# A seventh tap of the third channel block computed on ScalarE and GpSimd, one chunk late

## The reference

```
x = x + linear_attention(_gn(x))                 # layer 0
t = conv1x1(_gn(x), w_in)                        # layer 1, 384 channels
t = irfft2(rfft2(8x8 patches of t) * fft_filter)
t = depthwise_conv3x3(t, w_dw)                   # nine taps a channel
x = x + conv1x1(gelu(t[:192]) * t[192:], w_out)  # layer 1, end
```

## Time and profile before

| | |
|---|---|
| median of 3 runs | 3679.16 us (3678.93 to 3683.74) |
| the profiled execution | 3683.6 us, span 3681.8 us |
| mean granted TensorE clock | 0.977 |
| PE busy | 3441.9 us, 93% |
| DVE busy | 3143.5 us, 85% |
| POOL busy | 2025.3 us, 55% |
| ACT busy | 1658.8 us, 45% |

### The profile page before, as it was taken

How to read it: one execution, slowest core, us unless ns; L and a number is a source line. 1 busy time by engine, 2 the same in 40 slices (tenths; PEclk the granted TensorE clock), 3 DMA queues, 4 the chain that set the end, 5 groups by cost and what they waited for, 6 DMA issues and landing times.

```text
span 3681.8 us, 50526 instructions
## 1 busy us (share of the span) xinstructions
PE 3441.9 (93%) x17974; PEld 2995.9 (81%) x17974; DVE 3143.5 (85%) x4800; ACT 1658.8 (45%) x2834; POOL 2025.3 (55%) x1295
## 2 busy tenths in 40 slices
PE   4999999999999999999999999999999999999998
PEld 4987779877898778977789777897779977799775
DVE  7987989879898798987989869898798987989878
ACT  1433744337443374424744246442564325643265
POOL 2554655546555465564655646556465564655554
PEclk9999999999999999999999999999999999999999
DMA  6205232143321433123321233312332133321422
GB/s 216 69 26 172 100 115 70 38 160 112 104 69 60 146 114 110 61 69 129 129 95 61 87 123 120 101 59 95 121 121 95 52 121 109 115 87 52 145 95 95
DMA packets 185483, 369.92 MB, mean 100 GB/s; under 512 B 7915, under 2 KB 8979, under 8 KB 184979
## 3 DMA queue, kind: packets, MB, share of 16 engines
q1 hardware_dynamic: 185234, 366.68, 29.2%
HBM read 265.99 MB, written 100.66 MB: 100 GB/s over the span
## 4 chain that ended last, share of the span: by engine, by line
PE 32%; DVE 14%; issue 4%; POOL 2%; ACT 2%; DMA 0%; DVEq 0%; ACTq 0%; POOLq 0%; SPq 0%
DVE bank L970 6%; PE bank L1104 6%; PE bank L1103 6%; PE bank L1108 6%; PE bank L1133 2%; PE bank L1288 2%; PE bank L1261 2%; PE bank L1254 2%; DVE nrm L871 1%; DVE qt_lo L891 1%; PE bank L1121 1%; DVE xr L901 1%; PE bank L1273 1%; PE bank L1080 1%; DVE xr L904 1%
## 5 line engine op out<-in xcount | busy, mean ns | idle before, releaser
L445 POOL TENSOR_TENSOR t<-t 128x768 f32<-128x768 f32 x256 | 536.6, 2096 | 512.8 <-DVE t L807 512.8
L1103 PE MATMUL bank<-w_hi,x_hi 128*128 128x384 f32 x2304 | 778.9, 338 | 4.0 <-ACT x_hi L553 4.0
L1104 PE MATMUL bank<-w_lo,x_hi 128*128 128x384 f32 x2304 | 779.7, 338 | 0.0
L438 POOL TENSOR_TENSOR x_lo<-xa,x_hi 128x512 fp32r<-128x512 f32 x360 | 492.1, 1383 | 519.8 <-ACT x_hi L553 519.8
L970 DVE SCALAR_TENSOR_TENSOR bank<-big,wdw,bank 128x512 f32<-128x512 f32 x1072 | 753.8, 745 | 23.8 <-PE bank L1288 20.9
L558 ACT ACTIVATE t<-t 128x768 f32<-128x768 f32 x256 | 217.1, 848 | 867.9 <-POOL t L445 867.9
L510 POOL TENSOR_TENSOR prod<-prod 128x512 f32<-128x512 f32 x320 | 410.9, 1284 | 320.9 <-ACT prod L650 302.2
L817 DVE SCALAR_TENSOR_TENSOR kt<-t 128x384 f32<-128x384 f32 x256 | 534.9, 2090 | 0.0
L1108 PE MATMUL bank<-w_hi,x_lo 128*128 128x384 f32 x2304 | 533.1, 339 | 0.5 <-POOL x_lo L438 0.5
L1103 PEld LDWEIGHTS bank<-w_hi,x_hi 128*128 128x128 f32 x2304 | 434.7, 189 | 6.7 <-ACT x_hi L553 4.4
L1104 PEld LDWEIGHTS bank<-w_lo,x_hi 128*128 128x128 f32 x2304 | 433.8, 188 | 0.3
(11 more groups left out here) (132 smaller groups left out, 6969.9 us busy)
## 6 DMA issues: line engine op xcount, KB each, us to landing
xr<-x SPq DMA_DIRECT2D x128, 768.0 KB, 4.6
xa<-x SPq DMA_DIRECT2D x64, 768.0 KB, 6.3
x_scratch<-xr SPq DMA_DIRECT2D x64, 768.0 KB, 3.5
xa<-x_scratch SPq DMA_DIRECT2D x64, 768.0 KB, 6.1
xr<-x_scratch SPq DMA_DIRECT2D x64, 768.0 KB, 4.8
out<-xr SPq DMA_DIRECT2D x64, 768.0 KB, 3.5
big<-x SPq DMA_DIRECT2D x8, 768.0 KB, 10.0
w_raw<-wqkv_t SPq DMA_DIRECT2D x1, 1728.0 KB, 7.0
```

Source lines behind the costliest of these rows:

```text
L438: nc.gpsimd.tensor_tensor(dst, src, hi, ALU.subtract).then_inc(s_lo, 1)
L445: nc.gpsimd.tensor_tensor(a, a, b[:, :, ::-1, :], ALU.add).then_inc(s_add, 1)
L1103: nc.tensor.matmul(dst, hi(k), whi(k), start=first and k == 0, stop=False)
L1104: nc.tensor.matmul(dst, hi(k), wlo(k), start=False, stop=False)
```

## The change

The third block gets a seventh tap (q = 6) from ACT and POOL, and DVE begins it at (7,2). Tap 6 reads the row below the chunk, so its product cannot be formed in the step of the other six; it is formed at the start of the next step, on ACT by `product(c - 2, 6)` and on POOL by `add_product(c - 2, 6)`, both ahead of that step's other work. `copy_t` of tile 0 goes ahead of the products 0 to 2, and product 0, which overwrites slot 0, waits for tap (7,2) in place of (6,2). DVE's late taps are reordered.

```diff
-POOL_TAPS = 6
+POOL_TAPS = 7
-LATE = [(6, 2), (6, 0), (7, 2), (7, 0), (8, 2), (8, 0), (6, 1), (7, 1), (8, 1)]
+LATE = [(6, 0), (7, 0), (7, 2), (8, 0), (8, 2), (6, 1), (7, 1), (8, 1)]
-LAST = [(6, 2), (6, 0), (7, 2), (7, 0), (8, 2), (8, 0), (6, 1), (7, 1), (8, 1)]
+LAST = LATE
...
+                    if c >= 2:
+                        add_product(c - 2, 6)
                     if within(edge, 0, NCH, -1):
-                        for q in range(1, POOL_TAPS - 1):
+                        for q in range(1, 5):
                             add_product(c - 1, q)
...
-                            act.wait_ge(s_dw, dw_count(i, c - 1, (6, 2)))
+                            act.wait_ge(s_dw, dw_count(i, c - 1, (7, 2)))
...
+                    if gated:
+                        if c < NCH + 1:
+                            act.wait_ge(s_img, (i * 8 + c - 1) * 4 + 6)
+                        product(c - 2, 6)
+                    if tile:
+                        copy_t(T, 0)
                     if conv:
                         for q in range(3):
                             product(c - 1, q, edge == 1)
-                    if tile:
-                        copy_t(T, 0)
...
-                        for m, early in enumerate((LAST[0:2], LAST[2:4], LAST[4:6])):
+                        for m, early in enumerate((LAST[0:2], LAST[2:4], LAST[4:5])):
...
                         dve.wait_ge(s_img, T + 2)
-                        tap(c - 2, 6, 2)
                         tap(c - 2, 6, 0)
-                        tap(c - 2, 7, 2)
+                        tap(c - 2, 7, 0)
                     if 3 <= c <= NCH:
                         add_out(3, 2)
                     if gated:
-                        tap(c - 2, 7, 0)
+                        tap(c - 2, 7, 2)
+                        tap(c - 2, 8, 0)
                         tap(c - 2, 8, 2)
-                        tap(c - 2, 8, 0)
                         tap(c - 2, 6, 1)
```

More of the change, by code:

```diff
@@ L526, in part_c @@
                     if within(edge, 0, NCH, -1):
-                        add_product(c - 1, POOL_TAPS - 1)
+                        add_product(c - 1, 5)
                     if within(edge, 0, NCH if i + 1 < images else NCH - 1):
@@ L1014, in part_c @@
                             rope((i + 1) * NT, 0, 0)
-                        for q, k in LAST[6:]:
+                        for q, k in LAST[5:]:
                             tap(c - 2, q, k, last)
```

## The result

The changed kernel took 3673.25 us in the median of 16 runs (3664.39 to 3677.66), the kernel before 3680.36 us in runs beside them. The ratio is 0.9978, with a 95% interval of 0.997 to 0.9986: 0.22% faster, where 0.47% was forecast (3662.0 us). The profiled execution took 3674.24 us with a span of 3672.3 us, 9.5 us less than the span of before.

The account below looks back on a forecast made before the run. DVE was taken to set nearly the whole step of part C, with PE as floor near 17.8 us. 8 x (3.3 - 1.0 - 0.15) = 17.2 us off the median 3679.2 gave 3662.0 us; range 3654 to 3680, the forecast's own 3655 to 3671.

Parts of the forecast that it names:

- The steady step: Part C's repeating step, 18.67 us: a gain of 0.66 in each of five steps, 3.3 us an image.
- The ties: Four near-equal arrivals in the steady step, at (7,2), `gelu`, `copy_t` 3 and the output blocks, each reckoned to a tenth.
- the further 0.08 that I took off: Steady step: gain lowered from 0.74 to 0.66 us because four ties can only cost.
- the loop over product 6, POOL and the output block: Steady step: product 6, its add, (7,2), six POOL instructions and the output block form a loop of about 17.9 us.
- The lower bound of the range: 3654 us: a step gain of 0.9 with 0.8 lost at c = 2, 30 us in all.
- the 0.15 of the image's end: End of each image: the 4 us wait goes without a gain because `g_lo` ends 1.2 later; counted as -0.15 us.
- the 0.31 for the form with `prod`: Steady step: DVE's tap reading `prod` no longer runs beside POOL's `low_part`, 0.97 - 0.66 = 0.31 us gained.
- The step c = 2, up to `gelu`: First chunk: product 6 and its add delay the `gelu` table load; loss 1.34 or 0.8 us, mean 1.0 an image.
- Nothing behind gives it back: Step c = 2: the 1.34 us by which the `gelu` table load moves later is not recovered afterwards.
- The ties did not slip: Rival, chance 0.20: steady-step hand-overs cost 0.35 more or (7,2) stays long; only 4.8 us gained, 3674 us.
- DVE did bound the step before: Denies a rival, chance 0.05: PE's floor is higher, gain under 0.25 a step, time 3679 us.
- POOL did not make the step longer: Denies a rival, chance 0.15: POOL's chain behind product 0 becomes the bound, step 19.0 us, 21 us slower, 3700 us.

Follow-up runs that it names:

- The reorder alone: Kernel before with only DVE's late taps reordered, (6,2) second and (7,2) behind `add_out(3, 2)`, all nine taps kept on DVE: 3676.28 us, ratio 0.9997.
- The delay in the kernel before: Kernel before with three extra 128x512 copies on ACT ahead of each image's first `gelu`: 3704.95 us, ratio 1.0071.
- the filled gap in the changed kernel: Changed kernel with seven unread 128x512 matmuls on PE at c = 2, where it waits for the first `gelu`: 3656.34 us, ratio 0.9942.

## Why the prediction was off

**The steady step: right.** The sum came to 0.74 a step, I took 0.66, and the trace has 0.73 in the ordinary step and 0.80 at c = 7. The parts hold one by one: (7,2) at 3.32 (3.30) with 0.75 us and no wait, `times_filter` at 6.06 (5.95, and 6.02 for its transform), product 0 at 4.25 (4.2), `g_lo` at 13.7 (13.7). The ties cost no more than the sum had for them, so the further 0.08 that I took off was too much: 0.4 us an image. The agreement does not tell which engine sets the step now: the loop over product 6, POOL and the output block, put at 17.9 us under the rivals, is as long as the 17.94 measured. The lower bound of the range left out the 0.15 of the image's end (28.4 us in place of 30), which changes nothing here. The reorder alone confirmed the 0.31 for the form with `prod`.

**The step c = 2, up to `gelu`: right.** Forecast 1.0 in the mean, measured 1.14, with the wait of (7,2) for POOL at 0.58 us and the load of the table on the path behind the products.

**"Nothing behind gives it back": the step that failed.** I asked only whether the 1.34 us could be won back behind `gelu`, not whether PE's longer wait had a price of its own; the stretch behind `gelu` was put at nothing. PE's wait grew from about 0.4 us to between 1.67 and 2.61, and in six of eight images the clock fell to half behind it (PEclk 0.50): 1.6 us each, 9.4 in the whole. The delay in the kernel before and the filled gap in the changed kernel show it from both sides. In the second image over half of the longer wait comes from `copy_t` 0, which I had priced in the steady step and not at c = 2. With the gap filled, the ratio is 0.9942, 21 us; the forecast was 17.

In the profiled execution the 9.4 us stand for nearly the whole distance between the forecast 17.2 and the 9.5 by which the span fell. That is partly chance: the other misses (steps 3.6 us better than forecast, c = 2 up to `gelu` 1.1 worse, ends 3.0 worse, elsewhere 2.2 better) nearly cancel.

**The end of the image: near in seven, mis-sized in the last.** Forecast 0.15 an image, 1.2 in the whole; measured 0.2 in six images and 0.5 in one, but 4.2 in the whole. In the last image, where no next image gives PE work, the clock was already at half in parts before (PEclk 0.85 in the mean of the window) and the change prolonged it (0.81), which cost 2.55 us. In the other versions that keep the new order at the end, and have no matmuls added there, it was 0.7 to 1.3, so part of the 2.55 belongs to this execution.

**The rivals.** The ties did not slip, and DVE did bound the step before: with a tap less it is shorter. POOL did not make the step longer, but it now stands level with DVE: the chain runs over `prod` and `g_lo`, while PE is busy for 17.62 of 17.94 us. Two of its instructions are long at c = 7 (1.47 and 1.45 us beside `normalise`), at no cost to the step. One tap costs more there, 1.28 us on POOL and 0.71 on ACT against 0.66 on DVE, but that did not decide the time, since both had it free: in an ordinary step of 17.94 us POOL is busy for 14.03 and ACT for 14.59.

**Open.** The account leaves -2.2 us outside part C's marks, and 16 runs of the change spread over 13 us. A varying number of stretches at half the clock would make such a spread. The ten traces speak for it: the time outside the marks goes from 2507.1 us in the kernel with the copy moved, 83 of them at half the clock, to 2518.4 in the kernel before, 134 of them at half, and most of that time lies in parts A and B, which no edit touches. But each kernel was profiled once, so for the runs of one kernel it stays argued. Why `normalise` at c = 7 takes 3.50, 3.61, 4.17 or 4.25 us was not tried; other POOL instructions lie beside it in each case.

## What to carry to other kernels

Where a change makes TensorE wait longer at one place, price that wait twice, once for its length and once for a clock that falls behind it (here 1.6 us behind a wait of 1.85 to 2.61), and look in the trace for the matmuls that follow such waits. Take the cheap terms at the seams of a loop (the first and the last chunk, a table load) as seriously as the step that repeats: here the steady step gave 30 us, and leaving the first chunk as it was brought 20 us more on top of the change's own gain. A filler matmul in a gap, or one early activation that loads a table, is a cheap experiment, and here each was also a cure (13 and 17 us). It helps only where something waits for it: with the old order at c = 2 the early table gave nothing.

## What the runs showed of the hardware

- After a wait of TensorE of 1.85 to 2.61 us at c = 2, the granted clock fell from PEclk 1.00 to 0.50 in 14 of 14 cases (six images of the changed kernel, eight of the delayed one); after 1.25 to 1.74 us it stayed at 1.00 in 10 of 10 (two images, and eight of the kernel with the copy moved). The 4 us windows of the changed kernel show a mean of 0.57 to 0.65 or 1.00, and nothing between. These are the waits of this place alone, behind the same work.
- The wait was shortest in the two images that escaped, because PE had been slow ahead of it and came to it later: in the windows that end with `gelu` PEclk is 0.83 and 0.84 there (waits of 1.67 and 1.74 us), 0.85 to 0.88 in four others (1.85 to 2.04) and 1.00 in the last two (2.61). That a slow stretch ahead can spare the one behind it is read from these two images and was not tried.
- The tap of DVE that reads `prod` takes 1.05 us in the median of the kernel before (0.75 to 1.31), where it starts beside POOL's `low_part` in 47 of 64 cases, and 0.75 in all 64 cases both of the reorder and of the changed kernel, where it comes later in the step. Three `normalise` at c = 7 take 3.5 to 4.25 us in the four orders; why was not tried.
- The load of the `Gelu` table takes 1.28 us and comes once an image. At c = 2 of the changed kernel it lay on the path to `gelu`; moved to c = 0 it shows no cost (2514.5 us outside the marks, against 2516.2).
